# Pairs of groups from group 8 on in place of 12, in a conditioned gated feed-forward layer

## The chip, the cores and the metric

The kernel runs on one core of a Trainium2 chip. The metric is device time in microseconds. Three runs of the kernel before took 393.79, 394.14 and 395.14 us, median 394.14.

## What is computed

The reference, cut to what matters (x is 128 x 64 tokens of 256 values, the hidden layer 1024 wide; the weights up_w are 2048 x 256 and down_w 256 x 1024):

```
scale = cond @ norm_w.T + 1.0
ms = mean(x * x, axis=-1)
h = x * (scale[:, None, :] * rsqrt(ms + 1e-6))
val, gate = split(h @ up_w.T, 2, axis=-1)
h = val * gelu(gate)
s = 127 / max(|h|) per token
hq = clip(round(h * s), -128, 127) / s
wq = ternary(down_w * w) / w, with w = 1 / mean(|down_w|)
y = hq @ wq.T + x
```

## The kernel before, in words

The 8192 tokens are 64 groups of 128, four groups to a tile of x (a 512 KB load). For every group the hidden layer is made in two chunks j = 0, 1 of 512 columns, each with a GATE and a VAL part, so a group has two units u = 2g, 2g + 1. Precision comes from splitting: h and the weights are each a high and a low fp16 part, and a projection (`project`, L1090) is 6 matmuls of 512 columns: high by high, high by low and low by high, for two halves (k = 0, 1) of the 256 inputs. Groups 0 and 1 run in fp32.

**Pairs.** From group W0 = 12 to 59 two neighbouring groups are handled together (`pair`, L1120). Chunk 0 is done as ever, with four projections. Chunk 1 of the two groups is a 2 x 2 product of blocks, and is computed in 7 block products of 3 matmuls (`product`, L1106) in place of 8. For this a pair needs, beside its own four blocks (part 0 of `hp`), four sums and differences of blocks (part 1), made on POOL by `pair_sums` (L408), and four sums of weight blocks, `wt_hi` and `wt_lo`. These come once, by four steps each: `weight_sum` on POOL (L435), `weight_sum_high` on ACT (L609, the fp16 cast), `weight_sum_full` on ACT (L613, a scaled fp32 copy, written over the weights once all four sums are made), and `weight_sum_low` on POOL (L449), which raises `wt_ready`.

**The way of one pair.** DVE makes `hp` part 0 with `scale_h` (L809, twice, `pair_mul`), after `scale_rms` (L804) at the first group of a tile, which needs POOL's `rms_of` (L389) and thus ACT's four `squares`. POOL makes the sums (`pair_sum`). ACT casts each part to fp16 (`pair_high`, L566, `pair_hi`), POOL takes the rest (`pair_low`, L421, `pair_lo`), and SP turns each part with one transposing DMA into `hpT` (`turn_pair`, L298), which raises `own_loaded` for part 0 and `sums_loaded` for part 1. On PE, `pair(i)` waits for `own_loaded` and for all gelus of the groups before, does a product into ps_chainU (`u_ready`), a gate projection, the down projections due, and then waits for `u_copied`, `sums_loaded` and, in the first pair alone, `wt_ready` 4 (L1129 to L1132). ACT answers the first product with `pair_copy(i, 0)` (L575).

**What sets the order.** Each engine has its program written out by hand as a list of steps g = 2 to W0 - 1, then pairs, then steps 60 to 63; it is run strictly in that order. In step g PE does group g; ACT, DVE, POOL and SP prepare groups g + 2 and after, or, in the last two steps before W0, pairs 0 and 1. DVE's step (L1005) is: scale_h, combine of unit 2g - 1, the quantisation of group g - 3, combine of unit 2g. ACT's (L666): gelu of unit 2g - 1, the cast of group g + 2 or a pair_high, scale_downed, odd jobs, squares, gelu of unit 2g. In step 5 ACT also makes `dw_int`, from which DVE makes the ternary down weights (L952). POOL's (L486): low_part or the pair's work, sum_downed (the residual additions), rms_of, weight_sum, weight_sum_low. SP's (L350):

```
for g in range(F32G, W0):
    if g + AHEAD < W0:
        turn_h(g + AHEAD)
    elif g + 1 == W0:
        turn_pair(0, 0)
        turn_pair(0, 1)
    turn_quantised(g)
    loads(g)
```

so the first pair's transposes stand behind `turn_quantised` and `loads` of the step before. `loads(g)` (L334) issues the scale rows of a tile two ahead when g % 4 is 2 (for pairs 0), and x tiles 3, 4 and 5 in steps 4, 6 and 9.

Of the kernel before, what the change touches and what calls it, by code (L numbers as in the profile page):

```python
# [5 lines left out]
def cond_bitlinear_ffn(nc: bass.Bass, x, cond_norm, up_wT, down_wT, out):  # L6
# [19 lines left out]
    AHEAD = 2  # L26
# [1 line left out]
    XS, HS, QS, US, HA = 6, 3, 6, 3, 4  # L28
    DEQ, YS, LATE = 16, 4, 5

    W0, W1 = 12, 60
    NP = (W1 - W0) // 2
    NB = KD * 2
    EPS = 1e-6
# [8 lines left out]
    def quantised(g):  # L43

        return max(0, min(G, g - (2 if g < 20 else 1 if g < W1 else 0)))

    def downed(g):

        behind = 5 if g < 10 else 4 if g < W1 else 3 if g < G else 0
        return max(0, min(G, g - behind))  # L50
# [35 lines left out]
    with ctx:  # L86
# [301 lines left out]
        def _(pool):  # L388
# [32 lines left out]
            def pair_low(i, part):  # L421
                pool.wait_ge(pair_hi, 2 * i + part + 1)
                nc.gpsimd.tensor_tensor(hp_hl[:, i % 2, part, 1, :, :], hp[:, i % 2, part, :, :],  # L423
                                        hp_hl[:, i % 2, part, 0, :, :], ALU.subtract).then_inc(pair_lo, 1)
# [10 lines left out]
            def weight_sum(n):  # L435

                if n == 0:
                    pool.wait_ge(wlo_ready, 2)
                    pool.wait_ge(whi_ready, 2)
                    pool.wait_ge(val_ready, NJ * F32G)  # L440
                    pool.wait_ge(w_loaded[1][GATE], 16)
                    pool.wait_ge(w_loaded[1][VAL], 16)
                if n % 2 == 1:
                    pool.wait_ge(wt_sum, n)
                left, right = ((w_in[:, 1, VAL, 0, :], w_in[:, 1, GATE, 0, :]), (w_in[:, 1, VAL, 1, :], wt_raw[:, 0, :]),
                               (w_in[:, 1, VAL, 1, :], w_in[:, 1, VAL, 0, :]), (w_in[:, 1, GATE, 1, :], wt_raw[:, 1, :]))[n]
                nc.gpsimd.tensor_tensor(wt_raw[:, n, :], left, right, ALU.subtract).then_inc(wt_sum, 1)

            def weight_sum_low(n):  # L449
                pool.wait_ge(wt_scaled, n + 1)  # L450
                nc.gpsimd.tensor_tensor(wt_lo[:, n, :], wt_full[:, n, :], wt_hi[:, n, :], ALU.subtract).then_inc(wt_ready, 1)
# [26 lines left out]
            def sum_downed(g):  # L478
                for i in range(downed(g - 2), min(downed(g - 1), G - 1)):
                    sum_y(i)  # L480

            def next_rms(g):
                if g % NG == 1 and g // NG + 1 < NT:
                    rms_of(g // NG + 1)

            for g in range(F32G, W0):  # L486
                if g + AHEAD < W0:
                    low_part(g + AHEAD)
                else:
                    pair_sums(g + AHEAD - W0)  # L490
                    pair_low(g + AHEAD - W0, 0)
                    pair_low(g + AHEAD - W0, 1)
                sum_downed(g)
                next_rms(g)
                if 4 <= g < 8:
                    weight_sum(g - 4)
                if 7 <= g < 11:
                    weight_sum_low(g - 7)
            rms_of(W0 // NG + 1)
            for i in range(NP):  # L500
                g = W0 + 2 * i
# [20 lines left out]
        def _(act):  # L522
# [24 lines left out]
            def gelu(u):  # L547
                g, j = u // NJ, u % NJ
                if g < F32G:
                    act.wait_ge(rms_ready, 1)  # L550
                    scale = rms[:, 0, g:g + 1]
                else:
                    scale = comp[:, j, GATE:GATE + 1]
                if g == F32G:
                    act.wait_ge(comp_ready, j + 1)
                if u >= NJ * W1:

                    before = ((W1 - 2, 0), (W1 - 1, 0), (W1 - 2, 1))[u % US] if u < NJ * W1 + US else divmod(u - US, NJ)
                    act.wait_ge(h_ready, hs(*before))
                elif u >= US:  # L560
                    act.wait_ge(h_ready, u - US + 1)
                act.wait_ge(gate_ready, u + 1)
                nc.scalar.activation(gel[:, u % US, :], ps_gate[u % US][:, :], ACT.Gelu, scale=scale)\
                    .then_inc(gelu_ready, 1)

            def pair_high(i, part):  # L566
                if part == 0:
                    act.wait_ge(pair_mul, 2 * i + 2)
                else:
                    act.wait_ge(pair_sum, 4 * i + 4)  # L570
                if i >= 2:
                    act.wait_ge((own_loaded, sums_loaded)[part][i % 2], 16 * (i // 2))
                nc.scalar.copy(hp_hl[:, i % 2, part, 0, :, :], hp[:, i % 2, part, :, :]).then_inc(pair_hi, 1)  # L573

            def pair_copy(i, n):  # L575

                act.wait_ge(u_ready, 3 * i + n + 1)
                if n == 0:
                    act.wait_ge(gelu_ready, NJ * W0 + 4 * i - (2 if i else 0))
                    nc.scalar.copy(ps_one[:, :], ps_chainU[:, :]).then_inc(u_copied, 1)  # L580
                else:
                    if i >= 1:
                        act.wait_ge(val_added, 2 * i if n == 1 else 2 * i - 1)
                    nc.scalar.activation((u_two, u_three)[n - 1][:, :], ps_chainU[:, :], ACT.Copy, scale=comp[:, 1, VAL:VAL + 1])\  # L584
                        .then_inc(u_copied, 1)
# [23 lines left out]
            def weight_sum_high(n):  # L609
                act.wait_ge(wt_sum, n + 1)  # L610
                nc.scalar.activation(wt_hi[:, n, :], wt_raw[:, n, :], ACT.Copy, scale=recip[:, 3:4]).then_inc(wt_hi_ready, 1)

            def weight_sum_full(n):  # L613

                if n == 0:
                    act.wait_ge(wt_sum, 4)
                    act.wait_ge(wlo_ready, 4)
                    act.wait_ge(whi_ready, 4)
                nc.scalar.activation(wt_full[:, n, :], wt_raw[:, n, :], ACT.Copy, scale=recip[:, 3:4]).then_inc(wt_scaled, 1)
# [33 lines left out]
            def scale_downed(g):  # L653
                for i in range(downed(g - 2), min(downed(g - 1), G - 1)):
                    if i == G - 2:
                        last_take()
                    scale_y(i)
# [8 lines left out]
            for g in range(F32G, W0):  # L666
                gelu(NJ * g - 1)
                if g + AHEAD < W0:
                    high_part(g + AHEAD)
                else:  # L670
                    pair_high(g + AHEAD - W0, 0)
                scale_downed(g)
                if g == 3:
                    act.wait_ge(dw_loaded, 16)
                    nc.scalar.activation(dw_abs[:, :, :], dw[:, :, :], ACT.Abs, accum_out=dsum[:, :])\
                        .then_inc(dsum_ready, 1)
                if g == 5:
                    act.wait_ge(drec_ready, 1)
                    nc.scalar.activation(dw_int[:, :, :], dw[:, :, :], ACT.Copy, scale=drec[:, 0:1])\
                        .then_inc(dwint_ready, 1)  # L680
                if 6 <= g < 10:
                    weight_sum_high(g - 6)
                if 8 <= g < 10:
                    weight_sum_full(2 * (g - 8))
                    weight_sum_full(2 * (g - 8) + 1)
                if g % NG < 2:
                    squares(g // NG + 1, 2 * (g % NG))
                elif g + 2 >= W0:
                    squares(W0 // NG + 1, 2 * (g + 2 - W0))
                    pair_high(g + 2 - W0, 1)  # L690
                gelu(NJ * g)
            gelu(NJ * W0 - 1)
            for i in range(NP):
                g = W0 + 2 * i
                pair_copy(i, 0)
                scale_downed(g)
                pair_gelu(i, 0)
                pair_copy(i, 1)
                for n in range(quantised(g - 1), quantised(g)):
                    pair_quantise(n)  # L700
                pair_gelu(i, 1)
                pair_copy(i, 2)
                squares(g // NG + 2, g % NG)
                if i + 2 < NP:
                    pair_high(i + 2, 0)
                elif i + 2 == NP:
                    high_part(W1)
                pair_gelu(i, 2)
                pair_gelu(i, 3)
                if i + 2 < NP:  # L710
                    pair_high(i + 2, 1)
                elif i + 2 == NP:
                    high_part(W1 + 1)
                scale_downed(g + 1)
                for n in range(quantised(g), quantised(g + 1)):
                    pair_quantise(n)
# [601 lines left out]
```

## Time and profile before

| what | value |
|---|---|
| median of three runs | 394.14 us |
| the profiled execution | 394.78 us, of which the span from the first to the last instruction is 393.0 |
| PE, DVE, ACT, POOL busy | 98%, 81%, 70%, 56% of the span |
| granted clock of TensorE | 1.00 |
| DMA | 53.5 MB, mean 136 GB/s |

In the rows below times are microseconds from the span's start. A timeline row reads: start, length, engine, line, operation, output<-input, shapes, count, and in brackets the idle time before it with what ended it. Lengths of neighbouring rows of an engine overlap by some 0.1 us, since an instruction begins before the one before has written all; the distance between two starts is what an instruction takes of its queue.

### The profile page before, as it was taken

Reading aid. Unit: us, or ns where it says so; the run is one execution under the profiler, and the core shown is the slowest. Engines: PE = TensorE matmul, PEld = TensorE weight load, DVE = VectorE, ACT = ScalarE, POOL = GpSimd, SP = SyncE. Lnnn points to the kernel's source line nnn. Section 1 sums busy time; section 2 is a strip of 40 time slices with the busy share of each in tenths; the row PEclk is TensorE's granted clock in tenths of the full one; section 3 lists DMA queues with packets and bytes.
Section 4 is the critical chain, followed back from the end, with each engine's and each line's share of the span. In section 5 each row is a group of like instructions: output and inputs, shape, how many; then the busy total and the mean of one; then the engine's idle time right before and its main releaser. Section 6 shows DMA issues by size and latency. Waiting matters only on the chain.

```text
span 393.0 us, 6713 instructions
## 1 busy us (share of the span) xinstructions
PE 385.2 (98%) x2000; PEld 200.4 (51%) x2000; DVE 318.4 (81%) x653; ACT 274.7 (70%) x520; POOL 220.8 (56%) x298
## 2 busy tenths in 40 slices
PE   7999999999999999999999999999999999999994
PEld 4444454555455455545455554545555454554553
DVE  3698998978878897887987788798778879867983
ACT  3455648467887778788777878877787887675322
POOL 2142436876665578756565875656587565633202
PEclk9999999999999999999999999999999999999999
DMA  7265573578758578475965749585674566643442
GB/s 256 88 181 102 121 148 65 96 192 150 184 106 216 103 151 179 91 183 114 199 131 129 164 89 184 113 213 117 131 158 94 130 113 161 104 112 60 92 117 108
DMA packets 134076, 53.50 MB, mean 136 GB/s; under 512 B 125656, under 2 KB 129560, under 8 KB 134040
## 3 DMA queue, kind: packets, MB, share of 16 engines
q1 hardware_dynamic: 133752, 52.81, 61.3%
q8 instruction: 16, 0.26, 0.3%
q10 hardware_dynamic: 288, 0.26, 0.2%
q14 instruction: 20, 0.16, 0.1%
HBM read 13.60 MB, written 8.52 MB: 56 GB/s over the span
## 4 chain that ended last, share of the span: by engine, by line
PE 95%; DVE 2%; DMA 1%; issue 1%; ACT 1%; ACTq 0%; DVEq 0%
PE ps_y L1234 13%; PE ps_gate L1097 8%; PE ps_gate L1102 8%; PE ps_val L1100 8%; PE ps_val L1102 8%; PE ps_gate L1100 8%; PE ps_val L1097 8%; PE ps_gate L1110 6%; PE ps_gate L1112 6%; PE ps_gate L1111 6%; PE ps_val L1112 3%; PE ps_val L1111 3%; PE ps_val L1110 3%; PE ps_gate L1086 2%; PE ps_val L1086 2%; DMA cn_sb<-cond_norm 1%
## 5 line engine op out<-in xcount | busy, mean ns | idle before, releaser
L881 DVE TENSOR_REDUCE tmax<-act_h 128x1 f32<-128x1024 f32 x63 | 76.1, 1208 | 0.1
L600 ACT ACTIVATE gel<-ps_gate,comp 128x512 f32<-128x512 f32 x96 | 63.9, 685 | 14.8 <-PE ps_gate L1102 11.4
L460 POOL TENSOR_TENSOR y_out<-y_sc,x_sb 128x256 f32<-128x256 f32 x63 | 51.6, 822 | 24.3 <-ACT y_sc L631 17.4
L1234 PE MATMUL ps_y<-dw_q,qT 128*128 128x256 bf16 x504 | 64.7, 273 | 0.0
L606 ACT ACTIVATE q_int<-act_h,trec 128x1024 int16<-128x1024 f32 x49 | 56.3, 1149 | 7.4 <-DVE trec L1002 7.4
L414 POOL TENSOR_TENSOR hp<-hp 128x128 f32<-128x128 f32 x24 | 11.0, 458 | 84.7 <-DVE hp L824 84.7
L1234 PEld LDWEIGHTS ps_y<-dw_q,qT 128*128 128x128 bf16 x504 | 49.2, 98 | 17.9
L851 DVE SCALAR_TENSOR_TENSOR act_h<-ps_val,comp,gel 128x512 f32<-128x512 f32 x48 | 36.0, 751 | 25.6 <-PE ps_val L1102 24.3
L423 POOL TENSOR_TENSOR hp_hl<-hp,hp_hl 128x512 f16<-128x512 f32 x48 | 55.9, 1180 | 0.0
L1097 PE MATMUL ps_gate<-w_hi,hpT 128*128 128x512 f16 x96 | 36.4, 379 | 0.0
L1100 PE MATMUL ps_gate<-w_lo,hpT 128*128 128x512 f16 x96 | 36.4, 379 | 0.0
L1097 PE MATMUL ps_val<-w_hi,hpT 128*128 128x512 f16 x96 | 36.4, 379 | 0.0
L1100 PE MATMUL ps_val<-w_lo,hpT 128*128 128x512 f16 x96 | 36.4, 379 | 0.0
L901 DVE CAST q_bf<-q_int 128x1024 bf16<-128x1024 int16 x49 | 32.2, 658 | 4.1 <-ACT q_int L606 4.1
L631 ACT ACTIVATE y_sc<-ps_y,deq 128x256 f32<-128x256 f32 x63 | 30.0, 479 | 7.0 <-PE ps_y L1234 7.0
L573 ACT CAST hp_hl<-hp 128x512 f16<-128x512 f32 x48 | 29.4, 612 | 5.3 <-DVE hp L824 5.2
L432 POOL TENSOR_TENSOR act_h<-val_two,gel 128x512 f32<-128x512 f32 x24 | 32.8, 1366 | 0.0
L405 POOL TENSOR_TENSOR h_hl<-h,h_hl 128x256 f16<-128x256 f32 x14 | 10.1, 724 | 39.5 <-ACT h_hl L538 35.5
L863 DVE SCALAR_TENSOR_TENSOR val_one<-ps_val,comp,u_two 128x512 f32<-128x512 f32 x24 | 18.0, 750 | 16.3 <-PE ps_val L1112 16.3
L584 ACT ACTIVATE u_two<-ps_gate,comp 128x512 f32<-128x512 f32 x24 | 16.5, 687 | 18.6 <-PE ps_gate L1112 18.6
L530 ACT ACTIVATE squares_out<-x_sb 128x256 bf16<-128x256 f32 x64 | 25.8, 408 | 4.9 <-DMA x_sb<-x 4.9
L1102 PE MATMUL ps_val<-w_hi,hpT 128*128 128x512 f16 x96 | 28.6, 379 | 0.0
(145 smaller groups left out, 849.2 us busy)
## 6 DMA issues: line engine op xcount, KB each, us to landing
x_sb<-x SPq DMA_DIRECT2D x15, 512.0 KB, 4.7
out<-y_out SPq DMA_DIRECT2D x15, 512.0 KB, 3.4
w_in<-up_wT SPq DMA_DIRECT2D x4, 512.0 KB, 6.8
scale_tok<-scale_dram SPq DMA_DIRECT2D x15, 128.0 KB
dw<-down_wT SPq DMA_DIRECT2D x1, 1024.0 KB, 5.8
qT<-q_bf SPq DMA_TRANSPOSE x63, 3.1
hpT<-hp_hl SPq DMA_TRANSPOSE x48, 3.3
out<-y_out SPq DMA_DIRECT2D x4, 128.0 KB, 2.9
```

The costliest lines, as they stand in the source:

```text
L423: nc.gpsimd.tensor_tensor(hp_hl[:, i % 2, part, 1, :, :], hp[:, i % 2, part, :, :], hp_hl[:, i % 2, part, 0, :, :], ALU.subtract).then_inc ...
L460: nc.gpsimd.tensor_tensor(y_out[:, t % 2, n, :], y_sc[:, g % YS, :], x_sb[:, t % XS, n, :], ALU.add)\
L600: nc.scalar.activation(gel[:, place, :], bank[:, :], ACT.Gelu, scale=comp[:, n % 2, GATE:GATE + 1])\
L606: nc.scalar.activation(q_int[:, g % 2, :], act_h[:, g % HA, :, :].rearrange("p j c -> p (j c)"), ACT.Copy, scale=trec127[:, g % 2:g % 2 + ...
L851: nc.vector.scalar_tensor_tensor(act_h[:, g % HA, 0, :], ps_val[m][:, :], comp[:, 0, VAL:VAL + 1], gel[:, m, :], ALU.mult, ALU.mult).then_ ...
L881: nc.vector.tensor_reduce(tmax[:, i:i + 1], act_h[:, g % HA, :, :], AX.XY, ALU.max, apply_absolute_value=True).then_inc(tmax_ready, 1)
L1097: nc.tensor.matmul(bank[:, :], parts[:, 0, k, :], w_hi[:, j, s, k, :], start=(k == 0), stop=False)
L1100: nc.tensor.matmul(bank[:, :], parts[:, 0, k, :], w_lo[:, j, s, k, :], start=False, stop=False)
L1102: ins = nc.tensor.matmul(bank[:, :], parts[:, 1, k, :], w_hi[:, j, s, k, :], start=False, stop=(k == KD - 1))
L1110: nc.tensor.matmul(bank[:, :], left[:, 0, :], hi, start=start, stop=False, skip_group_check=not start)
L1111: nc.tensor.matmul(bank[:, :], left[:, 0, :], lo, start=False, stop=False, skip_group_check=not start)
L1234: ins = nc.tensor.matmul(ps_y[g % 2][:, 0:D], qT[:, g % QS, f, :], dw_q[:, f, :], start=(f == 0), stop=(f == NF - 1))
```

## The change

W0 goes from 12 to 8, so there are 26 pairs in place of 24, and groups 8 to 11 are done as pairs. SP, DVE and PE keep their code; what they do in steps 10 and 11 is done in steps 6 and 7. On POOL weight_sum moves from steps 4 to 7 to steps 2 to 5, weight_sum_low from steps 7 to 10 to steps 5 to 7 and after the last step. On ACT weight_sum_high moves from steps 6 to 9 to steps 3 to 5 (twice in 5), weight_sum_full from steps 8 and 9 to 5, 6, 6 and 7. The casts of pairs 0 and 1 are put elsewhere: pair_high(0, 0) and pair_high(1, 0) behind the gelus that end steps 6 and 7, pair_high(0, 1) near the start of step 7, and pair_high(1, 1) behind pair_copy(0, 0), in the first pair.

```diff
-    W0, W1 = 12, 60
+    W0, W1 = 8, 60
...
                     pair_low(g + AHEAD - W0, 1)
+                if g < 6:
+                    weight_sum(g - 2)
                 sum_downed(g)
                 next_rms(g)
-                if 4 <= g < 8:
-                    weight_sum(g - 4)
-                if 7 <= g < 11:
-                    weight_sum_low(g - 7)
+                if g >= 5:
+                    weight_sum_low(g - 5)
+            weight_sum_low(3)
             rms_of(W0 // NG + 1)
...
                     high_part(g + AHEAD)
-                else:
-                    pair_high(g + AHEAD - W0, 0)
+                elif g + 1 == W0:
+                    pair_high(0, 1)
                 scale_downed(g)
...
-                if 6 <= g < 10:
-                    weight_sum_high(g - 6)
-                if 8 <= g < 10:
-                    weight_sum_full(2 * (g - 8))
-                    weight_sum_full(2 * (g - 8) + 1)
+                if 3 <= g < 6:
+                    weight_sum_high(g - 3)
+                if g == 5:
+                    weight_sum_high(3)
+                    weight_sum_full(0)
+                if g == 6:
+                    weight_sum_full(1)
+                    weight_sum_full(2)
+                if g == 7:
+                    weight_sum_full(3)
                 if g % NG < 2:
                     squares(g // NG + 1, 2 * (g % NG))
                 elif g + 2 >= W0:
                     squares(W0 // NG + 1, 2 * (g + 2 - W0))
-                    pair_high(g + 2 - W0, 1)
                 gelu(NJ * g)
+                if g + 2 >= W0:
+                    pair_high(g + 2 - W0, 0)
             gelu(NJ * W0 - 1)
             for i in range(NP):
                 g = W0 + 2 * i
                 pair_copy(i, 0)
+                if i == 0:
+                    pair_high(1, 1)
                 scale_downed(g)
```

## Rows read from the trace of the kernel before

**Rows 1.** The page: busy time of PE, and its granted clock in 40 slices

```profile
PE 385.2 (98%) x2000; PEld 200.4 (51%) x2000; DVE 318.4 (81%) x653; ACT 274.7 (70%) x520; POOL 220.8 (56%) x298
...
PEclk9999999999999999999999999999999999999999
```

**Rows 2.** Waits of PE, the longest after its first instructions: total us, times, longest

```profile
PE ps_gate L1214 <- DVE q_bf L909: 0.5, 1, 0.5
```

**Rows 3.** Timeline of PE: starts of groups 8, 10, pairs 0, 1

```profile
57.97 0.38 PE L1097 MATMUL ps_gate<-w_hi,hT 128*128 128x512 f16 x1
...
70.07 0.38 PE L1097 MATMUL ps_gate<-w_hi,hT 128*128 128x512 f16 x1
...
83.05 0.38 PE L1110 MATMUL ps_gate<-w_hi,hpT 128*128 128x512 f16 x1
...
85.87 0.38 PE L1110 MATMUL ps_gate<-wt_hi,hpT 128*128 128x512 f16 x1
...
94.51 0.38 PE L1110 MATMUL ps_gate<-w_hi,hpT 128*128 128x512 f16 x1
```

**Rows 4.** Timeline of ACT, steps 5, 6 and 8

```profile
43.81 0.67 ACT L563 ACTIVATE gel<-ps_gate,comp 128x512 f32<-128x512 f32 x1
...
47.88 0.72 ACT L611 ACTIVATE wt_hi<-w_in,recip 128x512 f16<-128x512 f32 x1
...
59.21 1.32 ACT L619 ACTIVATE w_in<-w_in,recip 128x512 f32<-128x512 f32 x2
```

**Rows 5.** Timeline of DVE, steps 6 and 10

```profile
45.93 1.08 DVE L806 TENSOR_SCALAR rms_s<-rms,recip 128x4 f32<-128x4 f32 x1
...
49.74 0.76 DVE L904 TENSOR_SCALAR q_int<-act_h,trec 128x1024 int16<-128x1024 f32 x1
50.60 0.43 DVE L909 CAST q_bf<-q_int 128x1024 bf16<-128x1024 int16 x1
...
68.80 1.12 DVE L806 TENSOR_SCALAR rms_s<-rms,recip 128x4 f32<-128x4 f32 x1
...
73.04 1.36 DVE L904 TENSOR_SCALAR q_int<-act_h,trec 128x1024 int16<-128x1024 f32 x1
74.50 1.19 DVE L909 CAST q_bf<-q_int 128x1024 bf16<-128x1024 int16 x1
```

**Rows 6.** Timeline of SP's queue (SPq): DMA issues of steps 6 and 10

```profile
52.98 0.47 SPq L273 DMA_DIRECT2D x_sb<-x  x1
53.56 2.58 SPq L294 DMA_TRANSPOSE hT<-h_hl  x1
...
75.72 1.24 SPq L311 DMA_TRANSPOSE qT<-q_bf  x1
77.02 0.61 SPq L287 DMA_DIRECT2D scale_tok<-scale_dram  x1
77.68 3.86 SPq L303 DMA_TRANSPOSE hpT<-hp_hl  x2
```

**Rows 7.** Landing: all of L303; its first, at 77.68; all of L294 (hT)

```profile
DMA to landing us min/median/max: 3.1/3.3/5.1
...
DMA to landing us min/median/max: 4.5/4.5/4.5
...
DMA to landing us min/median/max: 2.4/2.4/4.8
```

**Rows 8.** ACT and POOL, durations: in ns min/median/max, or from the timeline

```profile
72.77 0.62 ACT L573 CAST hp_hl<-hp 128x512 f16<-128x512 f32 x1
...
83.90 0.57 ACT L580 COPY ps_gate<-ps_gate 128x512 f32<-128x512 f32 x1 [1.96 <-PE ps_gate L1112]
...
53.22 0.72 POOL L460 TENSOR_TENSOR y_out<-y_sc,x_sb 128x256 f32<-128x256 f32 x1
...
L423 POOL TENSOR_TENSOR hp_hl<-hp,hp_hl x4: 1157/1385/1613, 72.7 to 81.0; 128x512 f16<-128x512 f32 x4
...
L451 POOL TENSOR_TENSOR wt_lo<-w_in,wt_hi x4: 1150/1246/1436, 60.0 to 76.2; 128x512 f16<-128x512 f32 x4
```

## The prediction

> **What bounds the kernel now.** I read the busy shares first. TensorE (PE) is busy 98% of the span, and its granted clock is full in all 40 slices [rows 1]. The waits of PE come next: once it has started, the longest is 0.5 us, near the end [rows 2]. The timeline of PE then shows groups 2 to 11 and the first pair running with no gap. So a matmul that goes is worth its full time, and any wait put on PE costs its full length, because nothing later has slack to give back.
>
> **What the change takes away.** In an ordinary step a group has 24 matmuls of 512 columns. A pair has 45 for two groups, since its second chunk does 7 products of 3 in place of 8. Groups 8 and 9 take from 57.97 to 70.07, 12.10 us, with two down projections; the first pair, also with two, takes 83.05 to 94.51, 11.46 us [rows 3]. (A down is 0.87, so a matmul of 512 columns is (12.10 − 1.74) / 48 = 0.216 us.) A pair saves 3 of them, 0.64 us. Two pairs more (groups 8, 9 and 10, 11) save **1.3 us**, which is all there is to win: 0.33%, hardly over the 0.3% that a measurement of this kernel can tell from no change.
>
> **What it moves: 25 us less of preparation.** The first pair now starts at 57.97, where PE reaches group 8, and not at 83.05. Before it PE needs hpT part 0 (own_loaded), and 2.82 us into it, after one product, one projection and one down (83.05 to 85.87 [rows 3]), it needs part 1 and all four weight sums (wt_ready 4).
>
> *Edit 1, weight sums two steps earlier on POOL.* Four subtractions of about 1.3 us go into steps 2 to 5, where POOL mostly waits for ACT's casts; they stand behind low_part of their step, so the hT transposes don't move. Cost nothing; if that cover were gone, each next transpose of hT would be 1.3 us later, and PE never waited for one of them [rows 2].
>
> *Edit 2, ACT in step 5.* Behind the 2 us cast to dw_int come two weight_sum_high and one weight_sum_full, and only then squares(2,2) and gelu(10). ACT worked without a pause there up to gelu(10) at 43.81; one such activation takes 0.62 us of its queue (0.72 long, less the 0.1 by which neighbours overlap; two of the other kind 1.32) [rows 4], so three put 1.86 us ahead. PE doesn't wait for that gelu yet: its bank is wanted again only three units later. But DVE does (combine(10)), and POOL's rms of tile 2 needs the squares. DVE's scale_rms(2) moves from 45.93 [rows 5] to 47.79, and only behind it can hp of groups 8 and 9 be made.
>
> *Edit 3, when part 0 of pair 0 lands.* DVE runs in step 6 what it ran in step 10 before: scale_rms, two scale_h, a combine and a whole quantise, from 68.80 to the end of the cast at 75.69, 6.89 us, beside the same work on POOL (a weight_sum_low, four sums, two lows) [rows 5]. From 47.79 this gives q_ready for group 3 at 54.68. In SP's queue turn_q(3) and the loads of step 6 stand ahead of turn_pair(0,0), which is issued in step 7. The transpose of q holds SP 1.30 us, the scale 0.66 [rows 6], and, other than in step 10, a 512 KB load of x (load_x(4)) 0.58. So turn_pair(0,0) is issued at about 54.71 + 2.54 = 57.25. To landing, such a transpose took 3.3 us at the median, 4.5 behind a scale load (that very one, before), and 5.1 at most; the one transpose of hT behind a scale and an x load (53.56 [rows 6]) took 4.8, the most of its line and 2.4 above its median [rows 7]. I take 5.1, since an x load is in front: it lands at 62.35. PE waits from 57.97: **4.4 us**. Lower bound: the quantise runs undisturbed (q_int and cast in 1.29 us, from 49.74 to 51.03, in place of 2.65, from 73.04 to 75.69 [rows 5]) and the transpose takes 3.3: 59.2, a wait of 1.2. Upper bound: 3.3 + 2.4 = 5.7 to landing, 62.95, a wait of 5.0. pair_low(0,0) itself is done by about 53, so the queue, not POOL, is last. Part 1 follows in SP's queue 2.5 us later, lands at some 63.5, and PE wants it at 65.2: covered.
>
> *Edit 4, the cast pair_high(1,1) goes behind pair_copy(0,0).* This puts a ring of waits around the weight sums. pair_copy(0,0) needs PE's first product of pair 0. POOL in step 7 has pair_low(1,1), which needs that cast, and behind it in the same queue sum_y(0), weight_sum_low(2) and weight_sum_low(3). PE's second product waits for the last of these. So wt_ready 4 can't come before: product to copy's start 0.85 (83.05 to 83.90 [rows 3, 8]), 0.48 to the next on ACT (0.57 less the overlap), the cast 0.62 and 0.05 to POOL, a pair_low 1.3, a sum_y 0.7, two weight_sum_low of 1.25, and 0.1 back to PE [rows 8] = 6.6 us after the pair's start. PE gets there in 2.82. The second wait is **3.8 us**; with the least and the most of the POOL rows (1.16 and 1.61, 1.15 and 1.44) it is 3.4 to 4.7. It counts from where the pair really starts, so the first wait doesn't hide it. The squares and sum_downed that keep their places, and the third weight_sum_full, are off this chain.
>
> *What is late next.* rms of tile 3 is behind weight_sum_low(3) on POOL, so it comes about 1.3 us after the second wait; scale_h(12), (13) and pair_add(0,1) on DVE follow within another 3 us, and PE wants val_added about 8 us after that wait (a pair's 11.46 less 2.82 and the last product's 0.65). turn_pair(1,1) can be issued about 3.4 us into the pair, over 10 us ahead of pair 1. combine(15), for which ps_val[0] now waits, is done at about 62.8. I cost these at nothing; their cover is 2 us or more each. From pair 1 on everything stands as before.
>
> **The sum** is 4.4 + 3.8 − 1.3 = +6.9 us. The profiled execution took 394.78 (span 393.0 and 1.8 around it), 0.6 above the median of 394.14. Its own sum is 401.7; on the median it is **401.0 us**. The bounds add to 1.2 + 3.4 − 1.3 = +3.3 (397.4) and 5.0 + 4.7 − 1.3 = +8.4 (402.5).
>
> **The clock.** In the whole profile PE, once started, never waits more than 0.5 us and the clock stays at its level of 2.4 GHz [rows 1, 2]; the new waits are longer than any pause shown. The Trainium skill, "TensorE: Matmul & The Clock Gate", section "HAM oscillation", has it that gaps in which TensorE idles for a few microseconds put its clock back to half; no run here shows it, and by that rule the sum would come out higher.
>
> **Rivals.** (a) *The clock falls in one of the waits* to 1.2 GHz. A product of three matmuls more (0.65 us) lies on the ring after the first wait; after the second, the 15 matmuls up to ps_two's product (3.2 us at the full clock, 15 at 0.216) would take twice that. Some 3 us more: 404; if it stays low through all of pair 0, up to 8.6 more. Against it: two short waits with work between. The page above speaks for it. (b) *The first wait is short*, under 2 us: the x load doesn't hold up the transpose, DVE isn't stretched. For it: both lower bounds are rows. The ring remains: 394.14 − 1.3 + 3.8 + 0 to 2 = 396.6 to 398.6. (c) *Faster*: both waits are covered, and 392.8 comes out. The place is PE's wait for wt_ready 4: it would have to be met 2.8 us into pair 0, and hpT to land before 57.97. Against it: POOL alone has 4.5 us of queue behind a cast that needs PE's first product. It would take my having misread an order of the queues. (d) *In between*, a ring half as long and part 0 on time: within 0.3%, or slower by less than (b).
>
> **How the numbers follow.** The forecast (both waits, full clock) has 0.57, (a) 0.20, (b) 0.16, (c) 0.03, (d) 0.04, of which 0.02 within 0.3%. The likeliest gives 401.0. The range takes in the forecast's bounds down to the upper part of (b), and (a) at its usual price: 398.0 to 404.2. Slower has 0.95.
>
> **What would show it.** In the profile after, PE's waits list DMA hpT at the first product, 3 to 5 us near 58, then POOL wt_lo at the second, 3.4 to 4.7 us, each once, and none in pair 1. A pair still takes 11.46 us. scale_rms(2) starts at 47.8, and turn_pair(0,0) at 57.2, behind an x load. If the first wait is missing, my landing time is wrong; if the second is missing, the ring is. If the clock's row shows less than full near 65, (a) holds.

## The result and the profile after

The changed kernel takes **402.36 us** (median of 4 runs, 401.90 to 403.94) against 394.06 before (4 runs): a ratio of 1.021, 95% interval 1.018 to 1.025. It is 8.3 us slower where 6.9 were forecast. The profiled execution took 401.90, its span is 400.1. Three of the four executions show a mean granted clock of 0.990 or 0.991, the profiled one 0.995.

The waits of TensorE (PE) after the change, in the columns of [rows 2]. The first two are new, and there is a third small one:

```profile
PE ps_gate L1119 <- DMA hpT<-hp_hl: 4.7, 1, 4.7
PE ps_gate L1119 <- POOL wt_lo L451: 2.6, 1, 2.6
...
PE ps_y L1243 <- ACT y_sc L632: 0.4, 1, 0.4
```

PE's timeline, as in [rows 3]. The rows are the last down before the first pair, the first product (62.57), a matmul of the same product, the down, the second product (69.46), and the starts of pairs 1 and 2:

```profile
56.82 1.04 PE L1243 MATMUL ps_y<-dw_q,qT 128*128 128x256 bf16 x8
62.57 0.61 PE L1119 MATMUL ps_gate<-w_hi,hpT 128*128 128x512 f16 x1 [4.71 <-DMA hpT<-hp_hl]
...
63.40 0.63 PE L1121 MATMUL ps_gate<-w_hi,hpT 128*128 128x512 f16 x1
...
65.82 1.04 PE L1243 MATMUL ps_y<-dw_q,qT 128*128 128x256 bf16 x8
69.46 0.38 PE L1119 MATMUL ps_gate<-wt_hi,hpT 128*128 128x512 f16 x1 [2.60 <-POOL wt_lo L451]
...
78.10 0.38 PE L1119 MATMUL ps_gate<-w_hi,hpT 128*128 128x512 f16 x1
...
91.03 0.38 PE L1119 MATMUL ps_gate<-w_hi,hpT 128*128 128x512 f16 x1
```

PE reaches the pair at 57.69 (56.82 and a down of 0.87). Groups 8 and 9 now take until 78.10, 20.41 us, where they took 12.10 [rows 3]: 4.88 us to the first product, 6.89 from there to the second in place of 2.82, and 8.64 as in the first pair of before (85.87 to 94.51 [rows 3]). Groups 10 and 11 take 12.93 in place of 12.98 (70.07 to 83.05 [rows 3]): the saving of 0.64 is eaten by the wait for y_sc, 0.43 idle and some 0.6 of the queue's time. The rest of the program is 0.2 us longer, and PE was 0.3 earlier at group 8. In all the last matmul starts 8.2 us later than before (395.48 against 387.28). The span is only 7.1 longer, since 5.7 us follow that matmul before and 4.6 after; over the profiles of the experiments this end takes 4.4 to 5.7 us. So profiles are compared below by PE's timeline.

The matmuls behind the first wait are 0.43 us apart (62.97, 63.40) and last 0.63, where those of before are 0.216 apart; from 65.39 on they are again as before. The granted clock tells why. The windows of the changed kernel (stretch, its length, busy time of PE, PEld, DVE, ACT and POOL with instructions, then the granted clock, DMA share and GB/s):

```profile
57.90:62.00 4.10, 0.00 (x0) 0.00 (x0) 3.96 (x8) 0.00 (x0) 1.06 (x1) 0.98 1.16 176
62.00:63.00 1.00, 0.43 (x2) 0.16 (x3) 0.93 (x5) 0.00 (x0) 0.00 (x0) 0.50 1.28 287
63.00:64.00 1.00, 1.00 (x4) 0.43 (x3) 0.05 (x1) 0.00 (x0) 0.00 (x0) 0.50 1.21 268
...
66.00:69.00 3.00, 0.86 (x8) 0.52 (x6) 0.00 (x0) 0.69 (x1) 3.00 (x4) 1.00 0.45 87
```

The clock fell to its level of 1.2 GHz at the end of the first wait, and was back at 2.4 GHz before the second. Before the change it was full throughout [rows 1]. This is the rule that the prediction took from the Trainium skill, "TensorE: Matmul & The Clock Gate", section "HAM oscillation", and the trace agrees with it. After the second wait, 2.60 us, the clock read 1.00.

The engines that set the two waits, in timelines of the changed kernel. SP's queue (compare [rows 6]), the landing of the first transpose of hpT, DVE's scale_rms(2), POOL's two lows of pair 0 (1.36 us each), then ACT and POOL of the ring:

```profile
55.55 0.61 SPq L287 DMA_DIRECT2D scale_tok<-scale_dram  x1
56.20 0.47 SPq L273 DMA_DIRECT2D x_sb<-x  x1
56.72 3.99 SPq L303 DMA_TRANSPOSE hpT<-hp_hl  x2
...
DMA to landing us min/median/max: 5.8/5.8/5.8
...
47.34 1.13 DVE L815 TENSOR_SCALAR rms_s<-rms,recip 128x4 f32<-128x4 f32 x1
...
51.24 2.72 POOL L423 TENSOR_TENSOR hp_hl<-hp,hp_hl 128x512 f16<-128x512 f32 x2
...
64.07 0.57 ACT L581 COPY ps_gate<-ps_gate 128x512 f32<-128x512 f32 x1 [6.89 <-PE ps_gate L1121]
64.55 0.62 ACT L574 CAST hp_hl<-hp 128x512 f16<-128x512 f32 x1
...
65.25 1.16 POOL L423 TENSOR_TENSOR hp_hl<-hp,hp_hl 128x512 f16<-128x512 f32 x1 [6.30 <-ACT hp_hl L574]
66.37 0.73 POOL L460 TENSOR_TENSOR y_out<-y_sc,x_sb 128x256 f32<-128x256 f32 x1
67.05 2.26 POOL L451 TENSOR_TENSOR wt_lo<-w_in,wt_hi 128x512 f16<-128x512 f32 x2
```

The ring can be read off: PE's product from 62.57, ACT's copy at 64.07, the cast behind it, POOL (6.3 us idle before) at 65.25 with four instructions until 69.3, and PE at 69.46. POOL stood idle through nearly the whole first wait with this work behind it in its queue.

### The profile page after: what moved, and what is told of

It reads as the page before. It is cut to its first block, busy times and chain, and to the rows that moved or that the text cites. A ratio compares the mean times of both kernels' runs of the same rounds, so it can differ in the third digit from the quotient of the medians.

```text
span 400.1 us, 6745 instructions
## 1 busy us (share of the span) xinstructions
PE 385.6 (96%) x1994; PEld 199.6 (50%) x1994; DVE 315.5 (79%) x655; ACT 282.8 (71%) x530; POOL 228.3 (57%) x308
## 4 chain that ended last, share of the span: by engine, by line
PE 85%; DVE 5%; issue 4%; ACT 2%; POOL 2%; DMA 1%; ACTq 0%; DVEq 0%; POOLq 0%
PE ps_y L1243 12%; PE ps_gate L1119 7%; PE ps_gate L1121 7%; PE ps_gate L1120 7%; PE ps_val L1111 7%; PE ps_val L1106 7%; PE ps_val L1109 7%; PE ps_gate L1111 6%; PE ps_gate L1109 6%; PE ps_gate L1106 6%; PE ps_val L1121 3%; PE ps_val L1120 3%; PE ps_val L1119 3%; PE ps_gate L1095 2%; PE ps_val L1095 2%
## 5 line engine op out<-in xcount | busy, mean ns | idle before, releaser
L601 ACT ACTIVATE gel<-ps_gate,comp 128x512 f32<-128x512 f32 x104 | 69.4, 685 | 16.3 <-PE ps_gate L1111 12.3
L860 DVE SCALAR_TENSOR_TENSOR act_h<-ps_val,comp,gel 128x512 f32<-128x512 f32 x52 | 39.1, 751 | 35.2 <-PE ps_val L1111 34.0
L607 ACT ACTIVATE q_int<-act_h,trec 128x1024 int16<-128x1024 f32 x53 | 60.9, 1149 | 7.5 <-DVE trec L1011 7.5
L423 POOL TENSOR_TENSOR hp_hl<-hp,hp_hl 128x512 f16<-128x512 f32 x52 | 60.0, 1168 | 6.6 <-ACT hp_hl L574 6.6
L1106 PE MATMUL ps_gate<-w_hi,hpT 128*128 128x512 f16 x104 | 39.9, 384 | 0.0
L1109 PE MATMUL ps_gate<-w_lo,hpT 128*128 128x512 f16 x104 | 39.7, 382 | 0.0
L1109 PE MATMUL ps_val<-w_lo,hpT 128*128 128x512 f16 x104 | 39.4, 379 | 0.0
L1106 PE MATMUL ps_val<-w_hi,hpT 128*128 128x512 f16 x104 | 39.4, 379 | 0.0
L581 ACT COPY ps_gate<-ps_gate 128x512 f32<-128x512 f32 x26 | 14.8, 570 | 24.8 <-PE ps_gate L1121 24.8
L1119 PE MATMUL ps_gate<-wt_hi,hpT 128*128 128x512 f16 x78 | 29.6, 379 | 2.8 <-POOL wt_lo L451 2.6
L1111 PE MATMUL ps_gate<-w_hi,hpT 128*128 128x512 f16 x104 | 30.9, 379 | 0.0
```

Source lines behind the costliest of these rows:

```text
L601: nc.scalar.activation(gel[:, place, :], bank[:, :], ACT.Gelu, scale=comp[:, n % 2, GATE:GATE + 1])\
L607: nc.scalar.activation(q_int[:, g % 2, :], act_h[:, g % HA, :, :].rearrange("p j c -> p (j c)"), ACT.Copy, scale=trec127[:, g % 2:g % 2 + ...
L1106: nc.tensor.matmul(bank[:, :], parts[:, 0, k, :], w_hi[:, j, s, k, :], start=(k == 0), stop=False)
L1109: nc.tensor.matmul(bank[:, :], parts[:, 0, k, :], w_lo[:, j, s, k, :], start=False, stop=False)
L1111: ins = nc.tensor.matmul(bank[:, :], parts[:, 1, k, :], w_hi[:, j, s, k, :], start=False, stop=(k == KD - 1))
L1119: nc.tensor.matmul(bank[:, :], left[:, 0, :], hi, start=start, stop=False, skip_group_check=not start)
```

## The experiments

Each kernel is the changed one with the edit shown. The ratio is to the kernel before, run on the same chip (its medians were 394.44 in the first four, 394.08 in the next four, 394.38 in the last two). The waits are those of the profiled execution.

| kernel | median us | ratio (95%) | wait for part 0 | wait for wt_lo |
|---|---|---|---|---|
| changed | 402.36 | 1.021 (1.018 to 1.025) | 4.7 | 2.6 |
| e1_cast_first | 400.50 | 1.015 (1.012 to 1.018) | 5.0 | none |
| e2_order_of_turns | 398.42 | 1.009 (1.006 to 1.012) | none | 3.4 |
| e3_x_load_later | 400.48 | 1.015 (1.012 to 1.019) | 3.3 | 2.3 |
| e4_sums_behind_gelu | 399.93 | 1.014 (1.011 to 1.017) | 3.5 | 1.6 |
| e5_cast_and_turns | 397.05 | 1.006 (1.003 to 1.009) | none | 3.1 |
| e6_lows_and_turns | 393.80 | 1.000 (0.997 to 1.002) | none | none |
| e7_downs | 393.33 | 0.998 (0.996 to 1.001) | none | none |
| e8_awake | 402.56 | 1.019 (1.014 to 1.025) | 2.6 | 3.2 |
| e9_gelu_first | 393.41 | 0.998 (0.995 to 1.000) | none | none |
| e10_awake_twice | 401.00 | 1.017 (1.013 to 1.021) | 0.4 | none |

In e8 and e10 PE does other work in a part of the waits, so the columns show only what is left of them. The profile of one execution can differ from the median: in e2 PE reached the first pair only at 59.93, 2.2 us later than in the changed kernel.

The theory was that two things hold PE at the first pair: SP's queue, in which part 0's transpose stands behind turn_q(3) and two loads, and the ring through PE, ACT and POOL. The rivals were that hp or the transposes are late by themselves, that POOL is simply overloaded, and that the clock makes the loss.

**e1_cast_first.** Is it the ring?

```diff
             gelu(NJ * W0 - 1)
+            pair_high(1, 1)
             for i in range(NP):
                 g = W0 + 2 * i
                 pair_copy(i, 0)
-                if i == 0:
-                    pair_high(1, 1)
```

> pair_high(1,1) ahead of the first pair_copy. My theory (a ring: PE's first product, that cast, four instructions of POOL, PE's second product): POOL is done with weight_sum_low(3) by about 63.5, ahead of PE, so the wait for wt_lo (2.6 us) goes entirely, the wait for hpT (4.7) stays, and about 399.7 us come out. The half-speed matmuls after the first wait stay, since they follow from that wait. Rival (POOL is simply overloaded before the first pair, and the cast's place matters little): a wait for wt_lo of over 1 us remains, 401 or more.

The wait for wt_lo is gone altogether, while the first stays. POOL in e1 starts what follows the cast during the first wait:

```profile
58.29 2.71 POOL L423 TENSOR_TENSOR hp_hl<-hp,hp_hl 128x512 f16<-128x512 f32 x2
60.96 0.90 POOL L460 TENSOR_TENSOR y_out<-y_sc,x_sb 128x256 f32<-128x256 f32 x1
61.83 2.26 POOL L451 TENSOR_TENSOR wt_lo<-w_in,wt_hi 128x512 f16<-128x512 f32 x2
```

So the cast's place made the second wait. From the first product to the second e1 takes 4.17 us (63.38 to 67.55, half-speed matmuls again, for 2.82 us of work at full clock) in place of 6.89, which is the 2.7 expected. From where PE reaches the pair to its last matmul it takes 335.2 us (58.18 to 393.37) in place of 337.8 (57.69 to 395.48), 2.6 less, although this transpose took 6.1 us to landing (5.8 in the changed kernel). The medians show a gain of 1.9 only. Between the two profiled executions a later arrival of PE (0.5 us) and a longer end (5.7 against 4.6) take back 1.6, so the missing 0.8 is within what executions differ by outside that stretch; more isn't known of it.

**e2_order_of_turns.** Is it SP's queue?

```diff
-                elif g + 1 == W0:
+                elif g + 2 == W0:
                     turn_pair(0, 0)
                     turn_pair(0, 1)
                 turn_quantised(g)
```

> The two transposes of pair 0 ahead of turn_quantised(6) and loads(6) in SP's queue. My theory (the queue's order, not the making of hp, made part 0 late): pair_lo 1 is up at 52.5, part 0 lands at 56, and the first wait of 4.7 us goes entirely; the ring then costs its full 6.6 us against 2.8 of work, a wait of 3.8 for wt_lo, longer than the 2.6 before; in sum about 397.3 us if the clock stays up through 3.8 us without matmuls, 398 to 399.5 if it falls there too. Rival (hp itself is late, or the transposes are slow by themselves): a first wait of 2 us or more remains, 399.5 or more.

The first wait is gone, and the second grew to 3.4 us idle. SP's queue in e2, the landing of its first row, and PE, whose clock fell as it set out again:

```profile
54.66 2.80 SPq L303 DMA_TRANSPOSE hpT<-hp_hl  x2
57.50 1.46 SPq L311 DMA_TRANSPOSE qT<-q_bf  x1
...
DMA to landing us min/median/max: 3.0/3.0/3.0
...
59.93 0.38 PE L1119 MATMUL ps_gate<-w_hi,hpT 128*128 128x512 f16 x1
...
66.33 0.38 PE L1119 MATMUL ps_gate<-wt_hi,hpT 128*128 128x512 f16 x1 [3.42 <-POOL wt_lo L451]
...
66.90 0.63 PE L1121 MATMUL ps_gate<-wt_hi,hpT 128*128 128x512 f16 x1
```

hp was ready in time, and a transpose with nothing in front of it lands in 3.0 us. Both rivals for the first wait fall. The median, 398.42, is in the branch in which the clock falls, and the mean clock is under 1.00 in all five executions (0.993 to 0.998).

**e3_x_load_later and e4_sums_behind_gelu.** What of the first wait is the load of x, and what the three activations ahead of gelu(10)?

```diff
-                if g in (4, 6, 9):
-                    load_x({4: 3, 6: 4, 9: 5}[g])
+                if g in (4, 7, 9):
+                    load_x({4: 3, 7: 4, 9: 5}[g])
```

> load_x(4) issued in step 7, behind the transposes of pair 0, in place of step 6. My theory: its issue (0.5 us) and its 512 KB in front of the transpose (5.6 to landing in place of about 4.5) make 1.6 to 1.9 us of the first wait, so that falls from 4.7 to about 3.0; about 400.6 us, or 0.3 less if the clock doesn't fall. Rival (a scale load and a transpose of q in front are enough to make the landing slow): the first wait falls by 0.5 alone, 401.9.

```diff
-                if 3 <= g < 6:
+                if 3 <= g < 5:
                     weight_sum_high(g - 3)
-                if g == 5:
-                    weight_sum_high(3)
-                    weight_sum_full(0)
...
                 gelu(NJ * g)
+                if g == 5:
+                    weight_sum_high(2)
+                    weight_sum_high(3)
+                    weight_sum_full(0)
```

> In ACT's step 5 weight_sum_high(2), (3) and weight_sum_full(0) stand behind gelu(10) in place of ahead of squares(2,2). My theory: scale_rms(2), hp and the quantise of group 3 are 1.8 us earlier, and the first wait falls from 4.7 to 2.9 or a little less; about 400.5 us. Rival (the first wait is set by the DMA queue or by DVE's own load, and not by when ACT made the squares): the wait changes by under 0.5, 402.

Both came near what the theory said: the first wait fell from 4.7 to 3.3 and 3.5. Counted from where PE reaches the pair, the transpose of e3 is issued 0.5 us sooner, and it lands in 4.9 in place of 5.8; that of e4 is issued 1.4 us sooner and lands in 6.0. In e4 scale_rms(2) no longer meets POOL's weight_sum_low (46.91 to 48.22), but the two hp do; the timeline of DVE in e4:

```profile
46.45 0.23 DVE L816 TENSOR_SCALAR rms_s<-rms,recip 128x4 f32<-128x4 f32 x1
46.71 1.78 DVE L834 SCALAR_TENSOR_TENSOR hp<-x_sb,rms_s,scale_tok 128x256 f32<-128x256 f32 x2
```

The two rows together take what they took in the changed kernel (0.23 + 1.78 against 1.13 + 0.88), and the q_int behind them takes 1.59 in place of 1.36, which is half of why only 1.4 of the 1.86 us arrive. e4's clock fell only after the first product, and its ring is 6.25 us (62.10 to 68.35).

e3 shows what a fall at the second wait costs. Its clock fell at both waits, though the second was only 2.3 us:

```profile
67.48 0.59 PE L1119 MATMUL ps_gate<-wt_hi,hpT 128*128 128x512 f16 x1 [2.27 <-POOL wt_lo L451]
67.86 0.63 PE L1120 MATMUL ps_gate<-wt_lo,hpT 128*128 128x512 f16 x1
...
77.72 0.38 PE L1119 MATMUL ps_gate<-w_hi,hpT 128*128 128x512 f16 x1
```

From the second product to pair 1 that is 10.24 us in place of 8.64, 1.6 more. e2 and e8, whose clock fell there too, take 10.33 and 10.20. The two executions of e3 with a mean clock of 0.990 took 401.28 and 401.38, the two at 0.995 and 0.996 both 399.69.

**e5_cast_and_turns.** Do the two cures add up?

The edits of e1 and e2 together.

> The edits of e1_cast_first and e2_order_of_turns together. My theory: both the ring and the wait for part 0 are gone, but in e1 the first wait hid what POOL still had to do. Without it, PE wants wt_ready 4 at 2.8 us into the pair, about 60.5, and POOL's queue (pair_low(1,0) to 59.0, then pair_low(1,1) 1.2, sum_y 0.7, two weight_sum_low of 1.15) is done at about 63.1: a wait for wt_lo of 2 to 2.6 us and about 395.5 us. Rival (the two edits' gains add up, 1.9 and 3.9 us of 402.4, and more, since the cold matmuls go): no wait for wt_lo, 393 us.

They don't. The first product of e5 comes at 57.71, POOL's queue ends at 63.6 (64.1 in e1), and now nothing hides that:

```profile
57.81 2.72 POOL L423 TENSOR_TENSOR hp_hl<-hp,hp_hl 128x512 f16<-128x512 f32 x2
60.49 0.90 POOL L460 TENSOR_TENSOR y_out<-y_sc,x_sb 128x256 f32<-128x256 f32 x1
61.35 2.27 POOL L451 TENSOR_TENSOR wt_lo<-w_in,wt_hi 128x512 f16<-128x512 f32 x2
```

The median, 397.05, is 1.6 above what I had expected: the wait is 3.1 and not 2 to 2.6, and pair 1 still waits for y_sc. In the profile the clock stayed up, but four of the twelve executions have a mean clock of 0.995 or 0.996, as a run with one fall has. So "POOL's load" was no rival to the ring but the next wait in line: with the ring open, the two weight_sum_low are still 3.1 us late because of where they stand in POOL's queue.

**e6_lows_and_turns.** The order on POOL and that on SP; ACT is left as the change has it.

```diff
                 else:
+                    if g + 1 == W0:
+                        weight_sum_low(2)
+                        weight_sum_low(3)
                     pair_sums(g + AHEAD - W0)
...
-                if g >= 5:
+                if 5 <= g < 7:
                     weight_sum_low(g - 5)
-            weight_sum_low(3)
```

beside the edit of e2.

> The order of turns of e2, and on POOL weight_sum_low(2) and (3) ahead of pair 1's sums; the cast pair_high(1,1) stays behind pair_copy. My theory: POOL is done with the weight sums at about 58, before PE wants them, the ring is cut at another place than in e1, and both waits are gone; what is left is the saving of six matmuls (1.3 us) less a wait of 0.4 to 0.6 for y_sc in pair 1, so 0.7 to 1.3 us below the kernel before, 393.0 to 393.6, clock full throughout. Rival (the cast behind pair_copy costs by itself, or pair 1's part 1 comes too late): a new wait of over 1 us on hpT in pair 1 or on wt_lo, no faster than the kernel before.

Both waits are gone with the cast still behind pair_copy. What e6 waits for:

```profile
PE ps_y L1245 <- ACT y_sc L634: 0.4, 1, 0.4
PE ps_gate L1121 <- ACT gel L566: 0.4, 1, 0.4
```

The second was not foreseen: the last gelu stands behind pair_high(1, 0), which waits for DVE. The rival's sign, a new wait of over 1 us, isn't there; its outcome, no faster than before, can't be ruled out (0.9995, 0.997 to 1.002).

**e7_downs and e9_gelu_first** take these two away, one after the other.

```diff
-        behind = 5 if g < 10 else 4 if g < W1 else 3 if g < G else 0
+        behind = 5 if g < 9 else 4 if g < W1 else 3 if g < G else 0
```

> e6_lows_and_turns, and the step in which two down projections are due is 9 in place of 10 (behind = 5 if g < 9). My theory: the wait of 0.4 us for y_sc in pair 1 is there because three downs and two scale_y fall into pair 1, and it goes: 0.4 to 0.6 us below e6, about 392.8. Rival: it moves into pair 0, where two downs follow each other at its end, and nothing changes.

```diff
                 gelu(NJ * g)
-                if g + 2 >= W0:
-                    pair_high(g + 2 - W0, 0)
+                if g + 2 == W0:
+                    pair_high(0, 0)
             gelu(NJ * W0 - 1)
+            pair_high(1, 0)
```

> e7_downs, and on ACT the last gelu (unit 15) ahead of the cast pair_high(1,0), which waits for DVE's hp until 57.2. My theory: in e6 and e7 the first matmul of pair 0 waited 0.4 us for that gelu; it goes, and with it all that PE waits for near the first pair but 0.2 us: 392.9 us, against the kernel before 0.997. Rival (PE then waits for part 0 or for pair 1's part 0, whose cast is 0.6 later): as e7, 393.3.

e7's wait for y_sc is 0.2 in place of 0.4, and stands in pair 0 now (at 70.09; pair 1 begins at 71.62), so the rival was half right. In e9 the wait for gelu is gone, and another of the same size stands in its place, for combine(15), the last unit's, whose bank pair 0 wants again:

```profile
PE ps_val L1109 <- DVE act_h L856: 0.4, 1, 0.4
PE ps_y L1246 <- ACT y_sc L634: 0.2, 1, 0.2
```

It was neither of the two outcomes that I had written down, and e9 is no faster than e7. The medians, 393.33 and 393.41, are 0.75 and 0.97 us below the kernel before on the same chips, but both intervals reach 1.000: with 12 runs each it is not shown that either beats the kernel before. In the profiles, from where PE reaches group 8 to its last matmul, e7 and e9 take 329.0 us and the kernel before 329.3 (57.97 to 387.28). So of the 1.3 us saved 0.3 is left there, and the small waits have the rest.

**e8_awake and e10_awake_twice.** What is the clock worth? PE transposes the identity (a small matrix product whose result nobody reads) while it would wait, into banks that are free.

```diff
+                if i == 0:
+                    pe.wait_ge(gelu_ready, NJ * g)
+                    keep_awake(20)
                 pe.wait_ge(own_loaded[i % 2], 16 * (i // 2 + 1))
```

> The changed kernel, and in PE's program 20 transposes of the identity, as at the start, between the last gelu and the wait for pair 0's part 0, into a bank that is free then: PE has about 4.7 us of work in the first wait. My theory: the clock stays at its level of 2.4 GHz over the first wait; the ring shrinks from 6.9 to 6.6 us, but the wait for wt_lo grows to 3.8, since PE is through with its 2.8 us of work sooner; the fall of the clock in the first wait had cost 0.3 us only, the rest was hidden in the second. In all 0.3 us less, 402.0, or 1 more where the clock now falls in the longer second wait. Rival (the half-speed matmuls are worth their full loss): about 400.9.

In e10 keep_awake(40), and ahead of the wait for wt_ready 4, after a wait for the last combine, 32 more.

> The changed kernel with PE kept at work in both waits: 40 transposes ahead of the wait for part 0 (0.12 us each, by the run before this one), 32 more ahead of the wait for wt_ready 4. My theory: the clock stays at 2.4 GHz throughout, the ring is 6.3 us in place of 6.9, and the 1.6 us that the half-speed matmuls cost after the second wait in the runs with a mean clock of 0.990 are gone: about 401.2 us, 1.2 below the changed kernel. So of its 8.3 us above the kernel before some 7 are the two waits. Rival (the clock is worth much more, a third or more of the 8.3): 399.6 or less.

PE's timeline in e8: the 20 took 2.35 us, not 4.7, so half of the first wait is left; the clock stayed up over it, and fell in the second wait instead, which was longer.

```profile
57.79 2.35 PE L1064 MATMUL ps_gate<-ident 128*128 128x128 f32 x20
62.69 0.39 PE L1119 MATMUL ps_gate<-w_hi,hpT 128*128 128x512 f16 x1 [2.55 <-DMA hpT<-hp_hl]
...
68.92 0.58 PE L1119 MATMUL ps_gate<-wt_hi,hpT 128*128 128x512 f16 x1 [3.25 <-POOL wt_lo L451]
69.30 0.63 PE L1120 MATMUL ps_gate<-wt_lo,hpT 128*128 128x512 f16 x1
```

The ring at full clock is 6.23 us here (62.69 to 68.92) in place of 6.89. What that saves, the fall in the second wait takes back: e8's 402.56 is no faster than the changed kernel, between the two values of the theory and not near the rival's 400.9.

In e10 every execution shows a mean clock of 1.000, and it takes 401.00, 1.4 us below the changed kernel, near the 401.2 of the theory and far from the rival's 399.6. So the clock makes about 1.4 of the 8.3 us. That is rough: the medians are of 4 and 6 runs on different chips, and the intervals of the two ratios overlap. It fits the profiles, in which a fall at the first wait costs 0.66 us on the ring and one at the second 1.6. The other 6.9 us are the two waits and the small one of pair 1, less the saving.

## Why the prediction was right, point by point

- **The saving** of two pairs, 1.3 us: right. A pair still takes 11.46 us (91.03 to 102.49). With both waits cured (e6, e7, e9) the medians are 0.3 to 1.0 us below the kernel before, which no interval clears.
- **The first wait**, forecast 4.4, measured 4.9 (4.71 idle). Its parts: scale_rms(2) at 47.34 (47.79 forecast; the whole run was 0.3 us ahead), the issue of turn_pair(0,0) at 56.72 (57.25), the landing 5.8 us behind an x load (5.1 taken, 5.7 the upper bound, so the landing was the part mis-sized). That SP's order, the x load and the three activations make it is shown by e2, e3 and e4, each with its share.
- **The second wait**, forecast 3.8 from a ring of 6.6: the ring was 6.89 at half clock and 6.23 to 6.4 at full (e8, e2). Measured from the work that it displaces it costs 6.89 − 2.82 = 4.1. That the forecast is only 0.3 off is in part luck: at the full clock that it assumed the ring is 0.2 to 0.4 shorter than its 6.6, and the fall of the clock added 0.66. Its upper bound was added wrongly: with 1.61 and twice 1.44 the ring is 7.3 and the wait 4.5, not 4.7, so the bound of the whole is 402.3. The ring as the cause is shown by e1. What the prediction didn't see is that POOL's queue alone would have held PE as well, once part 0 is on time (e5).
- **The clock** was the rival (a), at 0.20, and it came true: the forecast as worded (both waits, full clock) did not. Its price was the term that was mis-sized. I had put 3 us on it, from half-speed matmuls after the second wait; a fall there cost 1.6 (e2, e3, e8), since the clock was back after some 8 of the 15 matmuls counted there (at 70.7 in e3). For a fall after the first wait the prediction had 0.65 us on the ring, and that is what the profiled execution shows: half-speed matmuls lost 1.3 us there, and all but 0.66 fell into a wait that PE had anyway. Over the runs the price is about 1.4. Three of the four executions of the changed kernel have a mean clock of 0.990 or 0.991; e3, at 0.990 in its profile, shows two falls, so in those three it probably fell twice.
- **What I costed at nothing.** "From pair 1 on everything stands as before" was 0.6 us off: three down projections fall into pair 1, and one waits for y_sc. Cover of the weight sums of steps 5 and 6, of part 1, of val_added and of combine(15) held in the changed kernel: PE waits for none of them. That of combine(15) was lent by the two long waits: in e9, where they are gone, PE waits 0.4 us for it.

In the profile, where the last matmul is 8.2 us later, the sum of +6.9 was 1.3 short: 0.5 from the first wait, 0.3 from the ring, 0.6 from pair 1 and 0.2 from the pairs behind it, less 0.3 at the start. So two waits at the two places named, each near its size, make the loss, as forecast; the median's 402.36 against 401.0 is about the clock's 1.4, which the forecast did not include.

## What to carry to other kernels

When a program written out in steps is shifted, look first not at the work but at each queue in front of the first consumer: here a transpose whose data POOL had finished at about 52.6 stood in SP's queue until 56.7, and two small subtractions stood behind one that needed the consumer's own first result. Such a ring has to be counted from where the consumer really starts, so a wait ahead of it doesn't hide it; and curing one queue shows what the next would have cost, so the cures don't add. Before moving a bound engine's work for 0.3%, put the price of a single exposed wait beside it: either one here cost more than three times the whole gain.

## What was not expected of the hardware

- The length of a wait alone doesn't tell whether the clock falls. In the profiled executions it fell with idle times of 4.7 (the changed kernel), 5.0 (e1), 3.4 (e2), 3.5 (e4) and 3.25 us (e8), in e2 and e4 only when PE had set out again; it stayed up over 3.08 (e5), 2.6 (the changed kernel) and 2.55 (e8), and yet fell at both waits of e3, 3.3 and 2.3. What decides it here stays open. Half-speed matmuls of 512 columns are 0.43 us apart.
- Six transposes of the identity at the kernel's start take 1.54 us, 0.26 each, and twenty of the same in e8 at 57.79 take 2.35, 0.12 each. Matmuls of one shape show the same in the changed kernel: four take 3.78 us at first and 1.98 later.

```profile
6.68 3.78 PE L1095 MATMUL ps_gate<-w_in,hT 128*128 128x512 f32 x4
...
11.38 1.98 PE L1095 MATMUL ps_val<-w_in,hT 128*128 128x512 f32 x4
```

The profile reads a granted clock of 1.00 at all these places. That TensorE starts at half speed although it reads so would explain it; no run tests it.
- A transposing DMA of part 0 behind a scale load and a 512 KB load of x lands in 5.8 to 6.1 us (the changed kernel, e1, e4, e8), behind a scale load alone in 4.9 (e3; 4.5 before), with neither in front in 3.0 (e2).
